# Gated cross-attention and ternary FFN on one core: 16-bit projections, norm by four batches, attention turns of eight heads

## What is computed

```python
def xattn(x, context, mask, Wq, Wk, Wv, Wo):          # heads of 16
    q, k, v = split(x @ Wq), split(context @ Wk), split(context @ Wv)
    scores = einsum('bhid,bhjd->bhij', q, k) * 16 ** -0.5
    attn = softmax(where(mask, scores, -max), axis=-1)
    return merge(einsum('bhij,bhjd->bhid', attn, v)) @ Wo
x = x + tanh(g_xattn) * xattn(layernorm(x), ctx, mask, Wq, Wk, Wv, Wo)
x = x + tanh(g_ffn) * ffn(layernorm(x), ternary(W1), b1, ternary(W2), b2)
```

## Time and profile before

| | |
|---|---|
| median of 3 runs | 1668.31 us (1665.9 to 1672.3) |
| the profiled execution | 1668.12 us, span 1666.3 us |
| instructions | 48258 |
| attention stage | from about 49 to 1141 us, 64 groups |
| FFN stage | from about 1150 us |

### The profile page before, as it was taken

The page is one execution under the profiler, slowest core; times in us unless marked ns, Lnnn a source line. Parts: engine busy times, 40 slices in busy tenths (PEclk is TensorE's granted clock), DMA queues, the critical chain, the costliest instruction groups (busy, mean ns, idle before and its releaser), DMA issues.

```text
span 1666.3 us, 48258 instructions
## 1 busy us (share of the span) xinstructions
PE 1511.3 (91%) x14501; PEld 1010.6 (61%) x14501; DVE 1487.7 (89%) x4375; ACT 938.2 (56%) x1799; POOL 668.6 (40%) x813
## 2 busy tenths in 40 slices
PE   3899999999999999999999999997999999999998
PEld 2566666666666666666666666664666666666665
DVE  7799999999999999999999999987888888888886
ACT  2465656565656666566656565644555554555554
POOL 5355555455554545554555555452111111111111
PEclk9799999999999999999999999986999999999999
DMA  2333333333333333333333333311010110101101
GB/s 79 89 97 85 94 85 86 97 86 97 83 96 83 97 84 93 87 89 92 86 97 83 98 81 97 80 47 55 27 38 25 38 36 27 38 25 38 38 25 51
DMA packets 207471, 117.93 MB, mean 71 GB/s; under 512 B 24912, under 2 KB 207184, under 8 KB 207440
## 3 DMA queue, kind: packets, MB, share of 16 engines
q1 hardware_dynamic: 207440, 117.54, 26.1%
HBM read 32.53 MB, written 16.78 MB: 30 GB/s over the span
## 4 chain that ended last, share of the span: by engine, by line
PE 54%; DVE 26%; issue 13%; ACT 4%; DVEq 2%; DMA 0%; ACTq 0%
PE bank L1060 12%; PE bank L308 9%; PE bank L1090 5%; PE bank L1089 5%; DVE smax L745 5%; PE bank L332 4%; PE bank L315 4%; PE bank L299 4%; DVE xres L790 3%; DVE rstd L685 3%; DVE k L715 2%; DVE rstd L687 2%; PE bank L387 2%; DVE y L1047 2%; DVE rstd L678 2%
## 5 line engine op out<-in xcount | busy, mean ns | idle before, releaser
L915 POOL TENSOR_TENSOR probl<-prob 128x512 f16<-128x512 f32 x512 | 528.9, 1041 | 535.8 <-ACT prob L597 534.9
L597 ACT ACTIVATE prob<-bank,masks 128x512 f32<-128x512 f32 x512 | 345.2, 687 | 144.9 <-PE bank L367 144.9
L745 DVE TENSOR_REDUCE smax<-bank 128x4 f32<-128x512 f32 x512 | 348.1, 681 | 14.5 <-PE bank L332 10.6
L1076 DVE TENSOR_TENSOR hidl<-hid 128x512 f16<-128x512 f32 x256 | 226.9, 886 | 79.5 <-ACT hid L1071 78.8
L1071 ACT ACTIVATE hid<-bank,b_sb 128x512 f32<-128x512 f32 x256 | 175.9, 687 | 212.3 <-PE bank L1060 206.1
L1060 PE MATMUL bank<-y,w1T 128*128 128x512 f16 x1024 | 262.9, 379 | 29.9 <-DVE y L1047 28.4
L1154 POOL TENSOR_TENSOR xres<-xres,b2g 128x1024 f32 (+1 forms) x32 | 75.7, 2365 | 431.3 <-ACT yln L1024 413.4
L1089 PE MATMUL bank<-w2T,hid 128*128 128x256 f16 x1024 | 237.4, 273 | 1.4 <-ACT w2T L1004 1.4
L1090 PE MATMUL bank<-w2T,hidl 128*128 128x256 f16 x1024 | 237.3, 273 | 0.0
L332 PE MATMUL bank<-k_rows,q_rows 34*128 34x128 f16 x2048 | 228.0, 222 | 6.8 <-DMA q_rows<-smaxT 3.4
L367 PE MATMUL bank<-q_rows,k_rows 50*128 50x128 f16 x2048 | 204.4, 221 | 0.9 <-DMA q_rows<-smaxT 0.9
(11 more groups left out here) (90 smaller groups left out, 2555.7 us busy)
## 6 DMA issues: line engine op xcount, KB each, us to landing
q_rows<-q SPq DMA_DIRECT2D x512, 64.0 KB, 2.6
k_rows<-k SPq DMA_DIRECT2D x512, 64.0 KB, 2.5
xres<-in_x_dram SPq DMA_DIRECT2D x64, 256.0 KB, 2.7
out_dram<-ystage SPq DMA_DIRECT2D x32, 512.0 KB, 2.9
ctx_sb<-in_ctx_dram SPq DMA_DIRECT2D x64, 192.0 KB, 3.1
q_rows<-smaxT SPq DMA_DIRECT2D x128, 8.0 KB
w_raw<-in_L_ffn_W_dram SPq DMA_DIRECT2D x2, 1024.0 KB, 6.7
prob<-in_L_xattn_Wq_dram SPq DMA_DIRECT2D x1, 256.0 KB, 3.9
```

The source lines that it names most:

```text
L597: act.activation(prob[u][:], st_bank[u % 2][:], ACT.Exp, bias=0.0, scale=masks[g.parity][:, 2 + b:3 + b]).then_inc(exp_done, 1)
L745: dve.tensor_reduce(smax[:, b, u * UH:(u + 1) * UH], sm_bank[u % 2][:].rearrange("p (h j) -> p h j", h=UH), AX.X, ALU.max).then_inc(max_ta ...
L915: pool.tensor_tensor(probl[u][:], prob[u][:], prob[u][:].bitcast(BF16)[:, 1::2], ALU.subtract).then_inc(prob_split, 1)
```

## The change

1. **16-bit projections.** x, ctx, attn and the weights are split in two halves of 16 bits; three products (high·high, high weight·low data, low weight·high data) replace one fp32 product. Weights are scaled by 64 and split at the start (`high_weights` on ACT, `low_weights` on DVE). For x and ctx the high half is the upper 16 bits of the fp32 word where it lies, and POOL writes the low half over the lower 16 bits (`low_x`, `low_ctx`); PE transposes both halves, and one ACT copy of 1024 elements takes them out. For attn, ACT writes the high half and DVE the low one (`low_attn`). The context's 192 columns are cut in 96 + 96 and not in 128 + 64.
2. **Turns of eight heads.** `scores`, `take_max`, `exponentials` and `weigh` go by two turns a batch, each over two PSUM banks; there is one such pair of banks for rough and one for exact scores, where there were two single ones. `low_prob` still splits 512 elements at a time, twice a turn, now in place in `prob`.
3. **Norm by four batches.** DVE does the first four parts (`seed_x`) in even groups, for two groups together; POOL does the other steps (`root_x`).
4. **Padded matmuls.** Rough scores have 64 rows (34 before), exact ones 64 (50), weighing 48 columns (33).
5. `low_q` and `low_k` are one instruction each; `read_weighed` leaves its sums in PSUM; `add_attention` of batch(0)-2 stands behind `read_weighed` and `normalise`.

```diff
-        def load_x(sp, g):
+        def load_x(sp, half):
...
         def transpose_x(pe, g, tr_free):
...
-            pe.wait_ge(ln_done, 2 * (g.n + 1))
-            for k in range(KD):
-                for b in range(2):
-                    last = pe.transpose(tr_bank[:, k * T + b * S:k * T + (b + 1) * S],
-                                        xln[:, b, k * P:(k + 1) * P], ident[:])
+            pe.wait_ge(x_split, g.n + 1)
+            for part in range(2):
+                for k in range(KD):
+                    for b in range(2):
+                        o = ((part * KD + k) * 2 + b) * S
+                        last = pe.transpose(tr_bank[:].bitcast(F16)[:, o:o + S],
+                                            halves(xln[:, b, k * P:(k + 1) * P], part), ident16[:])
...
+        SPLIT = ((0, 0), (0, 1), (1, 0))
...
         def project_q(pe, g, m):
...
-                last = pe.matmul(pj_bank[:, m * T:(m + 1) * T], wq_sb[:, k, m * P:(m + 1) * P],
-                                 xlnT[:, k, :], start=(k == 0), stop=(k == KD - 1))
+                for i, (wp, xp) in enumerate(SPLIT):
+                    last = pe.matmul(by_batch(m), wq16[:, wp, k, m * P:(m + 1) * P],
+                                     typed(xT16[:, xp, k, :], xp).rearrange("p (b s) -> p b s", b=2),
...
-        def scores(pe, g, b, u, rough=None):
+        def scores(pe, g, b, t, rough=None):
...
-                pe.wait_ge(exp_done, n - 1)
-            for c in range(UH):
+                pe.wait_ge(exp_done, n)
+            for c in range(PH):
...
-                last = pe.matmul(st_bank[u % 2][:, c * S:(c + 1) * S],
-                                 k_rows[g.parity][0:SR, b, u * UH + c, :],
-                                 q_rows[g.parity][0:SR, b, u * UH + c, :], start=True, stop=True)
+                last = pe.matmul(st_banks[:, c * S:(c + 1) * S],
+                                 k_rows[g.parity][0:SK, b, t * PH + c, :],
+                                 q_rows[g.parity][0:SK, b, t * PH + c, :], start=True, stop=True)
...
+        def low_x(pool, g):
+            pool.wait_ge(ln_done, 2 * (g.n + 1))
+            x = xln[:].rearrange("p b d -> p (b d)")
+            pool.tensor_tensor(x.bitcast(F16)[:, 0::2], x, x.bitcast(BF16)[:, 1::2], ALU.subtract).then_inc(x_split, 1)
...
+        def low_attn(dve, n):
+            dve.wait_ge(attnT_high, n + 1)
+            dve.tensor_tensor(attnT16[:, 1].rearrange("p k t -> p (k t)"), tr_bank[:, 0:KD * S],
+                              attnT16[:, 0].rearrange("p k t -> p (k t)"), ALU.subtract).then_inc(attnT_split, 1)
...
         def dve_group(dve, g, left):
...
-            take_max(dve, g, 1, 2)
-            norm(8)
             if not first:
-                add_attention(dve, g.batch(0) - 2)
-            norm(9)
-            take_max(dve, g, 1, 3)
+                low_attn(dve, g.batch(0) - 2)
+            take_max(dve, g, 1, 1)
+            norm(0)
             round_max(dve, g, 1)
-            norm(10)
+            norm(1)
             low_max(dve, g, 1)
+            norm(2)
             if not first:
                 read_weighed(dve, g.batch(0) - 1, 1, 1)
+                norm(3)
                 normalise(dve, g.batch(0) - 1, 1, 1)
-            norm(11)
+                add_attention(dve, g.batch(0) - 2)
...
         def pool_group(pool, g, left):
             for b in range(2):
                 for u in range(UNITS):
                     low_prob(pool, g, b, u)
+                    k = b * UNITS + u
+                    if g.parity == 0 and left >= 4 and k >= 1:
+                        for i in range(2 * k - 2, 2 * k):
+                            root_x(pool, g.half + 2, i)
+                    if b == 0 and u == 0 and left >= 3:
+                        low_ctx(pool, g.after(3))
                     if b == 1 and u == 0 and left >= 1:
                         pick_masks(pool, g.after(1))
+                    if b == 1 and u == 1 and left >= 3:
+                        low_x(pool, g.after(3))
```

More of the change, by code:

```diff
@@ L63, in bass_gated_cross_attention_ternary_ffn @@
     RB = 64
-    RK = 34
+    RK = 64
     MOVES = 4
@@ L387, in weigh @@
                 pe.matmul(o, high, v, start=True, stop=False)
-                last = pe.matmul(o, probl[u][:, c * S:(c + 1) * S], v, start=False, stop=True)
+                last = pe.matmul(o, low, v, start=False, stop=True)
             last.then_inc(weighed, 1)
@@ L403, in project_out @@
                 pe.wait_ge(*busy)
[L404 removed]
+            pe.wait_ge(attnT_split, n + 1)
             for k in range(KD):
[L406 to L407 removed]
+                for i, (wp, xp) in enumerate(SPLIT):
+                    last = pe.matmul(tr_bank[:, 0:D], attnT16[:, xp, k, :], wo16[:, wp, k, :],
+                                     start=(k == 0 and i == 0), stop=(k == KD - 1 and i == 2))
             last.then_inc(projected, 1)
@@ L658, in ln_part @@
         def ln_part(dve, i, rows, step, base, ready):
-            n = len(rows)
-            half, y, t, shift = (rstd[:, k, 0:n] for k in range(4))
+            half, y, t = (rstd[:, k, :] for k in range(3))
             if i > 0:
@@ new lines, in dve_group @@
+            norm(6)
+            read_weighed(dve, g.batch(0), 0, 0)
+            norm(7)
+            normalise(dve, g.batch(0), 0, 0)
+            if not first:
+                low_attn(dve, g.batch(0) - 1)
+            if left >= 2:
+                low_k(dve, g2)
+            norm(8)
+            if left >= 1:
+                take_max(dve, g1, 0, 1)
+                round_max(dve, g1, 0)
+            norm(9)
+            if left >= 1:
+                low_max(dve, g1, 0)
+            norm(10)
@@ L866, in dve_group @@
+            read_weighed(dve, g.batch(0), 0, 1)
+            norm(11)
+            normalise(dve, g.batch(0), 0, 1)
+            if not first:
+                add_attention(dve, g.batch(0) - 1)
             norm(12)
             if left >= 1:
-                take_max(dve, g1, 0, 0)
+                take_max(dve, g1, 1, 0)
             norm(13)
-            if left >= 1:
-                take_max(dve, g1, 0, 1)
-            read_weighed(dve, g.batch(0), 0, 0)
-            normalise(dve, g.batch(0), 0, 0)
@@ L1011, in norm_y @@
             for i in parts:
-                if i == 3 and not (isinstance(g.half, int) and g.n == 0):
-                    dve.wait_ge(y_done, QB * g.n)
-                rows = [row_of(g.n * QB + b) for b in range(QB)] if i == 0 else (None,) * QB
+                if i == LN_PARTS - 2:
+                    if isinstance(g.half, int) and g.n == 0:
+                        dve.wait_ge(ln_done, B)
+                    else:
+                        dve.wait_ge(y_done, QB * g.n)
+                rows = [row_of(g.n * QB + b) for b in range(QB)] if i == 0 else ()
                 ln_part(dve, i, rows, y_step, g.n * (LN_PARTS - 1), y_ready)
```

558 lines of the change are left out of this document (323 added, 235 removed).

## The result

| | before | changed |
|---|---|---|
| median | 1668.42 us | 2015.71 us (2011.23 to 2029.53) |
| ratio | | 1.209 (1.205 to 1.214) |
| the profiled execution's span | 1666.3 us | 2015.4 us |
| first and last set of ctx transposes (64 sets) | 27.9 and 1091.5 us | 31.5 and 1442.6 us |

What follows compares the result with a forecast made beforehand. Bound: the chain of waits through a group, 16.83 us growing to 21.7. 1668 + 5 for the start + 297 over 61 groups = 1970 us; 61 x 3 for half clock gives 2153, say 2150, range 1960 to 2290.

Steps and rivals of the forecast that it cites:

- The loop of waits: Chain of waits through one group of two batches, closing on the ctx transposes: 16.83 us before, mean 21.7 forecast.
- The sum at full clock: Sections added with PE always warm: odd groups 20.4, even 23.0, mean 21.7 us; 1970 us in all; rival 1, chance 0.22.
- A: From the ctx transposes through both halves of q until the k projection may start: 2.95 us.
- C: From the scores' end to the x transposes, waiting for POOL's `low_x`: from 5.25 to 10.35 us, 11.25 in even groups.
- D: From the x transposes to the end of the v projection: 4.15 us.
- E: From v's end to the next ctx transposes: 5.06 us, plus 0.8 for stalls, in odd groups; 7.6 in even ones.
- The clock, +3 us a group: PE's granted clock falls to half in sections with long waits; two thirds of +4.45 us taken, giving 2153, say 2150.
- B: k projection and scores, with the wait for the maxima's DMA: ends 5.25 us after the ctx transposes start.
- half rate throughout: Rival 2, from the skill's rule: PE always cold, 26.1 us a group, 2240 us; chance 0.20.
- Groups of two lengths: Sign of being right: attention groups of two lengths, some 3 us apart, even ones longer (23.0 against 20.4).
- Padding at nothing: Padded rows and columns of scores and weighing given no effect either way, their column time lying under a weight load.
- what SP moves has 4 us more room: SP issued the same moves within 16.83 us, so it is no end at 21; moves for later groups gain 4 us.

Runs made afterwards that it cites:

- run 1: `low_x` moved right behind the last split of a group's first batch, on the changed kernel: 1932.2 us.
- run 2: Both additions into xres moved right behind the 1024-element maximum that precedes them, on the changed kernel: 1946.3 us.
- run 3: Early `low_x` and both early additions together, on the changed kernel: 1672.8 us.
- run 6: On run 3: POOL makes `low_ctx` at a group's end, and SP loads ctx ahead of x: 1658.5 us.
- run 7: On run 6: masks behind both splits of (1,0), root steps spread, the last four into the next group, `low_attn` ahead of `low_v`: 1782.7 us.
- run 8: Padding undone (34, 50, 33 for 64, 64, 48) on run 3: 1714.3 us.
- run 9: On run 7: SP's load of x waits for the norm one step of four batches earlier: 1587.6 us.
- run 10: On run 9: both additions also ahead of the 1024-element maxima: 1580.3 us.
- run 11: On run 10: seed statistics split two and two, maxima's rounding and low half ahead of other seed parts, `low_ctx` ahead of root steps: 1544.2 us.
- run 4: Changed kernel with unread products added on PE, 4 before the ctx transposes and 14 before the x transposes: 1982.5 us.
- run 5: Padding undone (34, 50, 33 for 64, 64, 48) on the changed kernel: 2059.6 us.
- run 12: Padding undone (34, 50, 33 for 64, 64, 48) on run 11, the fastest kernel: 1572.2 us.

## Why the prediction was right

**The loop of waits: right.** The bound moved to waits on `low_x` (POOL) and on the late addition (DVE). Runs 1 to 3 show both. With both gone the time is 1672.8, beside 1668.4 before; what the smaller work is worth came only with runs 6 to 11.

**The sum at full clock, 21.7 us a group and 1970 us: near, and some 1.0 us a group too high.** Its parts, each from groups where nothing else disturbed it: A to C in even groups 11.2 (forecast 11.25) where A ran at 1.00; in odd groups 10.22 to 10.33 (10.35) where the maxima's move left on time; D 4.02 in run 4 (4.15); E 5.01 and 6.87 (5.86 and 7.6). Added, this is 20.7. Most of the difference is E. The 0.8 us for stalls between DVE and POOL did not come in the intervals without a seed: at 627.84 rounding took 0.18 us and the low half of the maxima 0.17, while POOL stood waiting for a load of ctx. That run 4 took 1982.5, 12 above the sum, is luck: A at half rate and the late maxima added what E had too much.

**The clock, +3 us a group: mis-sized.** That term is the larger part of what put 2150 where 2015 came. By the same parts the half rate cost 1.7 us a group: 5.40 - 4.02 = 1.4 in D, and 1.9 in the 9 of 56 intervals whose A was cold, 0.3 on the mean. So D lost 1.4 of the 2.2 forecast for a cold D, and A and B, with 2.25, were cold far less often than taken. Two cold D and a warm A and B (busy time and clock):

```profile
618.73:624.40 5.67, 5.54 (x57) 4.25 (x59) 1.98 (x4) 2.65 (x4) 1.71 (x4) 0.56 0.01 1
640.00:645.70 5.70, 5.31 (x57) 3.79 (x59) 2.02 (x4) 2.65 (x4) 2.04 (x2) 0.57 0.13 38
629.41:635.00 5.59, 5.21 (x87) 4.10 (x88) 2.92 (x7) 4.72 (x9) 3.88 (x4) 1.00 0.55 106
```

By the rule of the Trainium skill, "TensorE: Matmul & The Clock Gate", section "HAM oscillation — how this bites in real kernels", waits between bursts bring the half rate back in every turn. The trace agrees: in each of the 56 intervals D ran at 0.50 to 0.66. It does not bear out the 2240 that I made of it, half rate throughout: the clock of E was 0.97 or more in 46 of the 56.

**C in even groups, 11.25: right where A was warm.** There the maxima are copied out 2.43 us behind the ctx transposes (forecast about 2.43), the exponential of (1,0) starts at 5.25 (5.25) and the x transposes start at 11.2. The 12.4 to 13.5 belong to the 9 groups whose A was at half rate, where the copy ended only at 3.6 to 3.9; in the one at 606.33 the exponential started 6.43 behind. What the forecast did not see is that POOL's splits and root steps of the turn before end at the same time as that exponential (6.42 and 6.36 in the warm groups, 613.93 and 613.87 in the timeline): by these times POOL's queue was as long as the chain up to that point, so that a shorter path on one of them alone could give nothing there.

**C in odd groups, 10.35:** 10.2 to 10.3 in 8 of 27 groups, 10.6 to 11.2 in the 19 where the maxima's move stood behind SP's moves of q and k.

**E: right for the mechanism, 0.8 too long.** In the intervals shown, D and E together took 10.68 without a seed (forecast 10.0) and 12.80 with one (11.75). That hides two errors: D was 1.5 longer than forecast at full clock, E 0.85 and 0.5 shorter.

**Groups of two lengths, 3 us apart: wrong.** Where A was warm, 21.5 to 21.7 us and 22.5 to 22.8 alternate over long stretches, about 1 us apart, and the longer ones start in the odd group. Root steps lie inside the even group, but the seed lies at its beginning, and so in the interval that starts in the odd group. I had added both to the even one, 11.25 + 4.15 + 7.6; the mean is not touched, the pairing is.

**Padding at nothing: wrong**, by 44 us. It was priced by its columns, and its worth is in the clock. The forecast of the clock had no term for it, so its miss and this one partly hide each other: without padding the kernel took 2059.6, nearer to 2150.

**SP: "what SP moves has 4 us more room".** True of its issue time, not of its waits. The load of x waited for the last root step (29.1 us in 400 of the changed kernel), and POOL for a late load of ctx in every second group (25.4 in 400). I had not costed that. Through the maxima's move behind it, it lengthens A to C in odd groups here and in runs 2 and 4; runs 6, 7 and 9 show what it can grow to.

**Start: +5, measured 3.6. Second stage: within 5 us**, 2 us shorter behind the last ctx transposes.

## What to carry to other kernels

Cutting the work of two full engines by a fifth (PE from 15.6 to 12.5 and DVE from 16.0 to 13.0 us a group, before and in run 11) brought nothing while a step that the loop waits for stood behind independent work on a third engine. For every new semaphore, list what stands ahead of its signal on the signalling engine and move those things behind it; do this for all late signals together, since one alone shows a fraction of what they give. When a step moves into a later group, look for every wait on it, the DMA queue's pacing waits first, because all transfers behind it move too.

## What was not expected of the hardware

TensorE's granted clock was higher with wider products at the same count of instructions: 64 rows for 34 and 50 and 48 columns for 33 made 0.83 of 0.71, 0.98 of 0.85 and 1.00 of 0.94, with 28 to 44 us gained (runs 5, 8, 12). Products whose results nobody reads did the same in long waits (run 4, 0.83 to 0.97), at no cost on the chain. The same step of clock is not worth the same: 0.14 of it gave 33 us net of 2015 (run 4), where A to C grew again, while 0.06 went with 28 of 1544 in the kernel with short waits (run 12).
